# Feature interaction on one core: lines transposed as four 64x64 products with the identity instead of one 128x128 transpose

## What is computed

```python
# feature: (2048, 200, 64) float32, weight: (200, 64, 64) float32
bilinear = jnp.einsum('bie,ied->bid', feature, weight)
out      = jnp.einsum('bid,bjd->bij', bilinear, feature)     # (2048, 200, 200)
```

## Time and profile before

| | |
|---|---|
| median of 3 runs | 1306.28 us (1301.26 to 1307.94) |
| the profiled execution's own time | 1306.27 us |
| its span, first to last instruction | 1304.5 us |
| mean granted TensorE clock | 0.987 |
| busy: PE, ACT, DVE | 1198.4, 1056.7, 925.6 us |
| moved by DMA | 439.58 MB, mean 337 GB/s |

### The profile page before, as it was taken

How to read it: one execution, slowest core, us unless ns; L and a number is a source line. 1 busy time by engine, 2 the same in 40 slices (tenths; PEclk the granted TensorE clock), 3 DMA queues, 4 the chain that set the end, 5 groups by cost and what they waited for, 6 DMA issues and landing times.

```text
span 1304.5 us, 56312 instructions
## 1 busy us (share of the span) xinstructions
PE 1198.4 (92%) x24384; PEld 1030.4 (79%) x24384; DVE 925.6 (71%) x1792; ACT 1056.7 (81%) x1185; POOL 247.1 (19%) x375
## 2 busy tenths in 40 slices
PE   5999999999989999999989989899998999889985
PEld 4788788887778878897778878788777887778864
DVE  0477677777777768677776777777766777677795
ACT  4898787987889877997879977799787987779964
POOL 2111111122211112111121211212121112111111
PEclk9999999999999999999999999999998999999998
DMA  9699999999999999999999999999999999999899
GB/s 243 208 354 358 335 339 345 356 348 363 325 349 347 357 347 344 345 354 351 347 351 337 335 325 347 357 354 330 360 351 316 347 325 345 322 341 347 311 345 318
DMA packets 266133, 439.58 MB, mean 337 GB/s; under 512 B 40608, under 2 KB 237216, under 8 KB 265888
## 3 DMA queue, kind: packets, MB, share of 16 engines
q1 hardware_dynamic: 222112, 317.90, 69.6%
q0 software_dynamic: 43776, 118.09, 28.4%
HBM read 108.13 MB, written 327.68 MB: 334 GB/s over the span
## 4 chain that ended last, share of the span: by engine, by line
PE 66%; DMA 14%; issue 6%; DVE 5%; ACT 5%; SPq 2%; ACTq 0%; POOLq 0%; DVEq 0%
PE ps L286 43%; DMA out_dram<-staging 12%; PE ps L255 12%; PE ps L268 11%; ACT staging L316 3%; DVE staging L316 2%; SPq L189 2%; DMA x<-feature_dram 2%; ACT bl L338 2%; DVE win L363 2%; DVE win L371 1%; DMA w<-weight_dram 1%; DVE win L370 1%; ACT xt L328 0%; SPq L179 0%
## 5 line engine op out<-in xcount | busy, mean ns | idle before, releaser
L286 PE MATMUL ps<-win,bl 64*64 64x200 f32 x16384 | 840.2, 339 | 60.1 <-ACT staging L316 35.3
L286 PEld LDWEIGHTS ps<-win,bl 64*64 64x64 f32 x16384 | 674.5, 175 | 152.4 <-issue 58.8
L316 ACT COPY staging<-ps 128x800 f32<-128x800 f32 x768 | 625.8, 868 | 164.9 <-PE ps L286 67.6
L316 DVE COPY staging<-ps 128x800 f32<-128x800 f32 x256 | 253.2, 989 | 207.8 <-PE ps L286 206.4
L363 DVE COPY win<-xt 128x400 f32<-128x400 f32 x512 | 282.9, 553 | 138.5 <-ACT xt L328 78.0
L338 ACT COPY bl<-ps 128x1024 f32<-128x1024 f32 (+1 forms) x208 | 305.1, 1467 | 36.8 <-PE ps L268 35.3
L231 POOL DMA_DIRECT2D out_dram<-staging x256 | 161.6, 631 | 890.5 <-DVE staging L316 541.9
L268 PE MATMUL ps<-xt,w 64*64 64x128 f32 x6400 | 235.8, 275 | 13.8 <-issue 12.0
L255 PE MATMUL ps<-ident,x 128*128 128x128 f32 x1600 | 224.3, 283 | 21.4 <-DMA x<-feature_dram 15.5
L328 ACT COPY xt<-ps 128x1024 f32<-128x1024 f32 (+1 forms) x208 | 212.1, 1020 | 36.6 <-PE ps L255 36.2
L255 PEld LDWEIGHTS ps<-ident,x 128*128 128x128 f32 x1600 | 175.1, 143 | 73.5 <-issue 65.5
(11 more groups left out here) (2 smaller groups left out, 0.2 us busy)
## 6 DMA issues: line engine op xcount, KB each, us to landing
out_dram<-staging SPq DMA_DIRECT2D x768, 400.0 KB, 6.3
x<-feature_dram POOLq DMA_DIRECT2D x96, 1024.0 KB, 8.9
out_dram<-staging POOLq DMA_DIRECT2D x256, 50.0 KB, 5.8
x<-feature_dram POOLq DMA_DIRECT2D x16, 256.0 KB, 5.8
w<-weight_dram SPq DMA_DIRECT2D x24, 128.0 KB, 6.8
w<-weight_dram SPq DMA_DIRECT2D x2, 64.0 KB, 6.2
```

The costliest lines, as they stand in the source:

```text
L286: last = nc.tensor.matmul(tile[64 * g:64 * g + 64, h ^ g, F * b:F * (b + 1)], lines_of_bl(n, h, g, R * ORDER[s // 2] + r), win[64 * h:64 * ...
L316: copy(staging[:, slot, PB * s % OCT:PB * s % OCT + PB].rearrange("p b h j -> p h b j"), tile_of("s", n, s)[:, :, 0:PB * F].rearrange("p h ...
```

## The change

One 128x128 transpose of a line becomes four products on the 64x64 quarters: half v of the batch and half h of the line's values, each with a 64x64 piece of the identity as the moving operand (64 columns). The instruction is an ordinary `matmul` and no longer a `transpose`. The results of the two halves v of the batch go to the two banks of the tile (before, the two groups g did), so the order of the elements in a tile changes, and ACT's copy at L328 reads them as one run of (v k) g (c r). The number of instructions per full step u goes from 8 weight loads and 8 products to 32 and 32. Waits, semaphores, the order of the steps, the copies' sizes and the transfers stay.

```diff
         def transpose_tile(n, u):
-            cells = tile_of("t", n, u)[:].rearrange("p g (k c r) -> p g k c r", c=C, r=R)
-            return cells[:, 0:len(cells_of(u))]
+
+            cells = tile_of("t", n, u)[:].rearrange("p v (k g c r) -> p v k g c r", g=2, c=C, r=R)
+            return cells[:, :, :, 0:len(cells_of(u))]
...
                 for g in range(len(cells_of(u))):
                     for c in range(C):
-                        fs = slice(2 * E * (C * (u % 2) + c), 2 * E * (C * (u % 2) + c + 1))
-                        last = nc.tensor.transpose(transpose_tile(n, u)[:, g, :, c, :],
-                                                   x[:, at % XSLOTS, g, fs], ident[:])
+                        for a in range(2):
+                            for v in range(2):
+                                h = a ^ v
+                                e = 2 * E * (C * (u % 2) + c) + E * h
+                                last = nc.tensor.matmul(transpose_tile(n, u)[64 * h:64 * h + 64, v, :, g, c, :],
+                                                        x[64 * v:64 * v + 64, at % XSLOTS, g, e:e + E],
+                                                        ident[64 * v:64 * v + 64, 64 * v:64 * v + 64],
+                                                        start=True, stop=True)
                 last.then_inc(transposed, 1)
...
-                nc.scalar.copy(group_of_xt(n, u), transpose_tile(n, u).rearrange("p g k c r -> p k g (c r)")
+                nc.scalar.copy(group_of_xt(n, u), transpose_tile(n, u).rearrange("p v k g c r -> p (v k) g (c r)")
```

## The result

The changed kernel took 1576.91 us, the median of four runs (1559.13 to 1580.74), against 1304.69 for the kernel before, timed beside it: a ratio of 1.206, 95% interval 1.196 to 1.216. The prediction was 1249 us, faster, with a range of 1216 to 1296. It is 21% slower.

What follows compares the result with a forecast made beforehand. It took the kernel as bound alternately by transfers and PE. PE's saving of 8.9 us a block became 5.4, of which 3.6 was kept: 1306 - 54 (15 blocks) - 3 (start) = 1249 us, range 1216 to 1296.

Steps and rivals of the forecast that it cites:

- New: 8 groups of four products of 64 columns: PE's count for a full step's transposes after the change, from which its new time of 0.45 us was priced.
- The price of a group: Four 64-column products on PE's quarters, claimed at 0.056 us from 0.87 ns a column.
- the set: A full step's transposes on PE, claimed to fall from 1.15 to 0.45 us, saving 0.70.
- 43 us: Estimated 54% of a 79.0 us block that PE paces; only there was PE's saving to shorten the run.
- two thirds: Chosen share kept of the 5.4 us a block gain, because transfers take part: 3.6 us a block, 54 in 15.
- at the start: The 47 us before the steady part, where the cheaper transposes were counted as saving 3 us.
- 0.2% of DMA time, 0.1 us a block: Whole cost given to 9,600 more instructions beside 56,312, priced as their queue's transfer time.
- rival 3: Instructions don't come fast enough, so PE stops at every set of transposes: 1370 us, slower; chance 0.07.
- ten stops in 208 bilinear steps: Argument against slow instruction supply: PE's stops at L268 were that few, 12.0 us in all, 1.2 each.
- what bounds the kernel: Opening analysis: the run alternates between stretches paced by transfers (46% of the time) and by PE (54%).
- The change of shape: PE's loss going from quarters to the whole array and back, 0.27 us a set, claimed to vanish.

Runs made afterwards that it cites:

- half_product: Changed kernel with two products per line on the 64x128 halves of the array in place of four on the quarters; 1451.02 us (1.111).
- wide_half: Changed kernel with every second line left out and products of 128 columns in place of 64, so half as many products; 1402.07 us (1.074).
- filler_12: Kernel before, transposes kept, with 12 added products of 4 columns ahead of each full step's transposes; 1392.46 us (1.068).
- after_quiet: Changed kernel writing one of three output transfers, one batch entry of eight, with feature loads from block 1 on cut to 64 of 2048 values per partition; 1203.71 us.
- before_quiet: Kernel before writing one of three output transfers, one batch entry of eight, with feature loads from block 1 on cut to 64 of 2048 values per partition; 1190.01 us.
- before_light: Kernel before with two of SP's three output transfers left out; 1196.28 us.
- after_light: Changed kernel with two of SP's three output transfers left out; 1360.29 us.
- half_transpose: Two transpose instructions per line on the 64x128 halves of the array, against the kernel before's 128x128 transposes; 1321.96 us (1.014).

## Why the prediction was wrong

**Two steps failed.** The first is "New: 8 groups of four products of 64 columns". A full step has 16 groups, for a float32 product is two matmuls with two weight loads. The rows that it rested on held this: L268 shows x32 for a bilinear step, for which the code issues 16 products, and L286 x16 for a score step of eight. I read the records as products and never set their count against the loops. The price of a group, 0.056, was right (0.058 measured); the set was 0.92 us and not 0.45, and saved 0.23 and not 0.70.

With that error alone put right, the prediction's own sum gives a small gain: 3.0 of 70.8 us of PE a block, 4.2% of 43 us, two thirds of it in 15 blocks, 18 us, and 1 at the start: 1287 us. With the 0.85 that half_product measured it is 195 x 0.23 x 0.85 = 38 us, 1268. Both are faster, and inside the range. **The step that decided** is therefore the second, the instructions, "0.2% of DMA time, 0.1 us a block". They were 22,400 more, not 9,600, and their price is not the time of their transfer but PE's stop until it is there: 306 us, or 20 us a block. With the count of 9,600 it would probably have failed too: wide_half and filler_12, with about that many more (231 blocks), took 1402 and 1392 us.

This was rival 3, given 0.07. Its mechanism is what happened: PE stops with nothing to wait for, decided by 0.70 us a set; measured were 306 us more over 208 sets, 1.5 us. They are not all inside the sets, as it had them: the most idle time is ahead of the scores, 125.1 us. Its price, 1370 us, was too low, for a stop took 344.4 / 193 = 1.8 us on the mean and not 1.2, a set saved 0.23 and not 0.70, and it forgot that the clock falls behind a stop.

"Against: ten stops in 208 bilinear steps" failed as an argument, because the kernel before stood at the threshold already: its blocks took 6.59 us on the mean, but the shortest 5.36, and its round trip was 5.49. One step of "what bounds the kernel" was missing, then: not PE or the transfers alone, but also PE's instruction stream, which those transfers delay. In the kernel before its stops took 38 us.

**What was right.** The change of shape is gone from the steps, as forecast: in the changed kernel the new products start between scores (219.84 in the timeline) without the 0.27 us. By the same reading the old transposes had a use: they were few instructions in much time, 16 in 1.15 us, and so gave the next block time to arrive. The new ones are 128 in 0.92.

**The pages.** The Trainium skill's page "TensorE: Matmul & The Clock Gate", section "Wait — 56ns, not 53.3ns?", has a floor of about 25 ns between starts. The trace disagrees: 64 starts in 0.92 us are 14 ns each, on quarters of the array. The Trainium skill's page "Runtime: NRT & Kernel Launch", section "Instruction fetch mechanics", says that an engine's instructions are brought in blocks of 16 KB (256 instructions) while the present ones run, the cost mostly hidden. The trace agrees on the block (281 packets for the places 256 apart) and not on the cost: 344 us of 1571.

**Shown and not shown.** Shown: the stops lie at every 256th instruction and end a fixed time after an instruction packet; the same instructions lose most of the stops (344 to 38 us) with nearly all other transfers gone; the instructions' number alone, without the change, brings them. Not shown: what starts the transfer of a block. That it is the beginning of the block before is read from the times (in after_quiet the start of the transfer scatters least about that point), not tried; in before_quiet a quarter of the transfers start shortly before it. Nor does the wait follow the rate of the other transfers alone: it was 1.00 us at 193 GB/s (before_light) and 1.67 at 170 (after_light). Nor is it tried whether another order of the same transfers would shorten the wait.

## What to carry to other kernels

Count an engine's instructions, not the calls in the code: set the xcounts of the trace against the loops before pricing an edit. In these traces a float32 product on TensorE is two pairs of instructions, and a transpose is one. Where a kernel keeps the DMA engines full, divide TensorE's instructions by 256 and see how much of its own work that leaves per block. Here it was 5.8 us before (16 x 70.8 over 194 blocks), 5.1 in half_transpose and 3.9 in the changed kernel, beside round trips of 5.1 to 5.7, and the gains in TensorE's work of the latter two came back as stops. Many short instructions were cheap here only beside nearly idle DMA engines.

## What the runs showed of the hardware that I had not expected

- TensorE's instructions arrive 256 at a time, and with the DMA at 281 to 337 GB/s a block's round trip was 4.6 to 5.7 us; with nearly no other transfers 3.6 us. A stop ended 1.37 to 1.42 us after the end of the packet, the medians of the ten runs that have more than a few stops.
- Four matmuls of 64 columns on the quarters of the array, weight loads included, took 0.058 us, so eight instructions in 58 ns are not too many when they are there.
- The matmuls of a float32 product of 128 stationary and 64 moving columns on half the array started about every 0.11 us for a pair of halves, where those of the transpose instruction of that shape started about every 0.06. A product has two of them and a transpose one: a step of 1.93 us against 0.64.
